# Attention, a ternary feed-forward and a channel mix in one launch: when stage one loads, sums and rounds its weights, and a loop in place of unrolled VectorE code

## The reference

```python
# x: (8, 512, 512), ctx: (8, 512, 384)
v = ln(x) @ Wv.T + bv;  t = ctx @ Wt.T + bt              # 512 x 256 each
x = x + (v @ t.T) / max(|v| |t|.T, 1e-8)                  # cosine attention
h = act_quant(ln(x)) @ ternary(w1).T                      # 512 -> 2048
h = silu(depthwise_conv3(h, conv_w) + conv_b)
x = x + act_quant(h) @ ternary(w2).T                      # 2048 -> 512
x = x + softmax_attention(ln(x), ctx)                     # 16 heads of 32
x = x + sigmoid(xr @ W_r.T) * (relu(xk @ W_k.T)**2 @ W_v.T)   # channel mix
```

## Time and profile before

| | us |
|---|---|
| median of 3 runs (1741.2 to 1742.52) | 1742.46 |
| the profiled execution: time | 1742.46 |
| its span, first to last instruction | 1740.7 |
| PE busy | 1591.3 (91%) |
| DVE busy | 1226.8 (70%) |
| ACT busy | 1159.6 (67%) |
| POOL busy | 1090.5 (63%) |
| mean granted TensorE clock, as a share of full speed | 0.975 |

### The profile page before, as it was taken

One profiled execution on the slowest core, in us unless ns is written; L12 is line 12 of the kernel. 1 busy time (PEld: TensorE's weight loads), 2 busy tenths in 40 slices (PEclk: granted clock), 3 DMA queues, 4 the chain that ended last, 5 costly groups with the idle time before them and its releaser, 6 DMA issues. The chain is left out here.

```text
span 1740.7 us, 29515 instructions
## 1 busy us (share of the span) xinstructions
PE 1591.3 (91%) x8932; PEld 718.5 (41%) x8932; DVE 1226.8 (70%) x1736; ACT 1159.6 (67%) x1915; POOL 1090.5 (63%) x786
## 2 busy tenths in 40 slices
PE   4989878998999977899999999999999978999998
PEld 2545433443444432334344444444443413444443
DVE  3888888988988755577686767676767674565553
ACT  4667598888888744665757666665757565656662
POOL 2767558888898833566757666675756673545452
PEclk9989999999999997999999999999999988999999
DMA  7321000000000113121211212121201100000001
GB/s 287 121 85 61 1 1 1 1 1 1 0 1 1 43 47 90 29 59 29 55 37 33 57 25 57 29 55 31 58 24 41 55 25 25 25 37 35 24 24 49
DMA packets 60464, 72.23 MB, mean 41 GB/s; under 512 B 14416, under 2 KB 40016, under 8 KB 59856
## 3 DMA queue, kind: packets, MB, share of 16 engines
q1 hardware_dynamic: 56944, 62.22, 12.1%
q10 hardware_dynamic: 3424, 8.91, 1.4%
HBM read 37.40 MB, written 8.39 MB: 26 GB/s over the span
## 5 line engine op out<-in xcount | busy, mean ns | idle before, releaser
L1540 DVE TENSOR_REDUCE s_mx<-bank 128x1 f32<-128x512 f32 x512 | 336.8, 685 | 199.9 <-PE bank L1672 194.1
L1425 ACT ACTIVATE s_E<-bank 128x512 f32<-128x512 f32 x512 | 293.5, 595 | 195.1 <-PE bank L1686 170.4
L1322 POOL TENSOR_TENSOR s_E<-s_E 128x1024 f32<-128x1024 f32 x128 | 300.4, 2366 | 121.5 <-PE bank L1694 113.8
L1672 PE MATMUL bank<-s_KA,s_QA 96*128 96x512 f16 x512 | 193.3, 388 | 16.9 <-DMA s_KA<-sm_cx 7.2
L1686 PE MATMUL bank<-s_QA,s_KA 97*128 97x512 f16 x512 | 196.0, 383 | 7.1 <-ACT s_E L1425 3.5
L1315 POOL TENSOR_TENSOR sm_cx<-s_qkf,sm_cx 128x512 f16<-128x512 f32 x64 | 76.4, 1194 | 175.0 <-ACT sm_cx L1403 174.1
L1694 PE MATMUL bank<-s_E,s_V 128*32 128x512 f32 x1024 | 138.0, 611 | 3.2 <-ACT s_E L1425 3.2
L1846 POOL TENSOR_TENSOR sm_cx<-m_xf,sm_cx 128x512 f16<-128x512 f32 x56 | 78.6, 1409 | 98.7 <-ACT sm_cx L1887 98.7
L1056 PE MATMUL bank<-sm_zz,w1raw 128*128 128x512 f16 x256 | 100.1, 391 | 27.0 <-DVE sm_cx L943 11.1
L1079 PE MATMUL bank<-f_w2q,w2raw 128*128 128x512 f16 x512 | 122.0, 379 | 1.4 <-ACT w2raw L824 0.6
L758 POOL TENSOR_TENSOR w1raw<-w1raw,sm_cx 128x512 f32<-128x512 f32 x88 | 121.0, 1384 | 2.3 <-ACT sm_cx L841 2.3
(11 more groups left out here) (262 smaller groups left out, 4116.9 us busy)
## 6 DMA issues: line engine op xcount, KB each, us to landing
sm_cx<-in_ctx SPq DMA_DIRECT2D x16, 768.0 KB, 4.6
s_QA<-sm_cx SPq DMA_DIRECT2D x384, 32.0 KB, 1.9
s_KA<-sm_cx SPq DMA_DIRECT2D x372, 32.0 KB, 1.9
X<-in_x SPq DMA_DIRECT2D x8, 1024.0 KB, 6.5
out_x<-X SPq DMA_DIRECT2D x8, 1024.0 KB, 4.3
w1raw<-in_w ACTq DMA_DIRECT2D x1, 4096.0 KB, 13.4
w2raw<-in_w ACTq DMA_DIRECT2D x1, 4096.0 KB, 28.3
w1raw<-in_wq SPq DMA_DIRECT2D x1, 1024.0 KB, 6.1
```

Source lines behind the costliest of these rows:

```text
L1322: e.tensor_tensor(into, into, other, ALU.add).then_inc(s_sum.sem, 1)
L1425: e.activation(E[:, SLOT[k] + h, :], SC[u % 2][:, :], ACT.Exp, scale=1.0 / float(np.sqrt(DH)))\
L1540: e.tensor_reduce(mx[:, q, h:h + 1], MX[q % 2][:, :], AX.X, ALU.max).then_inc(s_red.sem, 1)
L1672: e.matmul(MX[k % 2][:, :], QA[0:MROW, m, h, q * P:(q + 1) * P], KA[0:MROW, m, h, :], start=True, stop=True).then_inc(s_mx.sem, 1)
```

## The change

In `cosine_attention`: `cw` and `cb` are no longer loaded by SP at the start but by ACT, behind w1 and w2, and they count on w1's semaphore, so that every sum over w1 waits for 64 in place of 32. The sums are dealt out differently: one quarter of w1 in batch 0 (before two), one quarter and two eighths of w2 in batch 1, two quarters of w1 in batch 2. So w1's total falls to batches 2 and 3, and `weight_scale(0)` with `conv_scales` to batch 3, ahead of the first `quantised`. The statistics of the feed-forward's first batch move from the end of batch 2 to the end of batch 1. In batch 7 `rescale` moves from DVE to POOL (behind `split`, ahead of `add`), and ACT does two of its four `rescaled` behind `root_v`. In `softmax_attention` DVE's batches 1 to 6 become a loop.

```diff
-        SUMS = {0: ((0, 0), (0, 1)), 1: ((0, 2), (0, 3)), 2: ((1, 0),), 3: ((1, 1),), 4: ((1, 2),), 5: ((1, 3),),
-                6: ((1, 4),), B - 1: ((1, 5), (1, 6), (1, 7))}
-        QUANT, STATS_AT = {3: 0, 4: 1, 5: 2, 6: 3}, 2
+        SUMS = {0: ((0, 0),), 1: ((0, 1), (1, 0), (1, 1)), 2: ((0, 2), (0, 3)), 3: ((1, 2),), 4: ((1, 3),), 5: ((1, 4),),
+                6: ((1, 5),), B - 1: ((1, 6), (1, 7))}
+        QUANT, STATS_AT = {3: 0, 4: 1, 5: 2, 6: 3}, 1
...
-        s_raw, LOADED = [sem(f"raw{i}") for i in range(2)], 32
+        s_raw, LOADED = [sem(f"raw{i}") for i in range(2)], (64, 32)
...
-            e.dma_start(cw[:, :], cw_d).then_inc(s_bias, 16)      # SP
-            e.dma_start(cb[:, :], cb_d).then_inc(s_bias, 16)
...
+            e.dma_start(cw[:, :], cw_d).then_inc(s_raw[0], 16)    # ACT, behind w1 and w2
+            e.dma_start(cb[:, :], cb_d).then_inc(s_raw[0], 16)
...
+                else:                                             # POOL, batch 7
+                    for q in range(TT):
+                        rescale(q)
                 add(b)
...
-                    for q in range(TT):                           # ACT, batch 7
-                        rescaled(q)
+                    rescaled(0)
+                    rescaled(1)
                 root_v(b)
...
+                    rescaled(2)
+                    rescaled(3)
...
-                    e.wait_ge(s_raw[i], LOADED)                   # DVE, weights(b)
+                    e.wait_ge(s_raw[i], LOADED[i])
...
-                if b == 2:
-                    weight_scale(0)
-                    conv_scales()
                 if b in QUANT:
+                    if QUANT[b] == 0:
+                        weight_scale(0)
+                        conv_scales()
                     quantised(QUANT[b])
                 weights(b)
-                if b == 1:
+                if b == 2:
                     total(0)
...
-                    if b == 2 and i == 0:                         # PE
+                    if b == 3 and i == 0:
                         total(0)
...
-            steps(step, e, unrolled=True)                         # softmax_attention, DVE
+            steps(step, e)
```

More of the change, by code:

```diff
@@ L304, in centre, with rescale @@
                 e.tensor_scalar(nmr[:, :], nmr[:, :], -1.0, None, ALU.mult).then_inc(s_nmr.sem, 1)
+            def rescale(q):
+                s_r1.wait(e, 0, q + 1)
+                e.tensor_scalar(z[:, q, :], z[:, q, :], ROUND, rs1[:, q:q + 1], ALU.subtract, ALU.mult)\
+                    .then_inc(s_r2.sem, 1)
             ln_p(e, 0)
@@ L371, in _ @@
             context(0)
-            e.wait_ge(s_bias, 64)
+            e.wait_ge(s_bias, 32)
             def rescaled(q):
@@ L432, in total @@
             def total(i):
-                e.wait_ge(s_ws, PARTS[0] if i == 0 else sum(PARTS) + 1)
+                e.wait_ge(s_ws, PARTS[0] + 2 if i == 0 else sum(PARTS) + 1)
                 lo = i * PARTS[0]
@@ L451, in quantised @@
                 piece = raw[0][:, i * F:(i + 1) * F]
-                e.wait_ge(s_ws, PARTS[0])
+                e.wait_ge(s_ws, PARTS[0] + 2)
                 e.tensor_scalar(piece, piece, wr[:, 0:1], 1.0, ALU.mult, ALU.min).then_inc(s_wt, 1)
@@ L464, in token_scales @@
                 e.reciprocal(s1[:, :], rs1[:, :]).then_inc(s_am.sem, 1)
[L466 to L469, removed]
             def low_f(c):
@@ L478, in reciprocals @@
                 e.reciprocal(NT[:, :], nt[:, :]).then_inc(s_rec.sem, 1)
-                if b == B - 1:
-                    for q in range(TT):
-                        rescale(q)
                 s_root.wait(e, b, 2)
@@ L580, in norms_v @@
                     s_sq.wait(e, b, 2 * KH)
-                    if b == 2:
+                    if b == 3:
                         e.wait_ge(s_wm, 1)
@@ L600, in total @@
             def total(i):
-                e.wait_ge(s_ws, sum(PARTS) + 2 if i else PARTS[0] + 1)
-                s_root.wait(e, B - 1 if i else 1, 2)
+                e.wait_ge(s_ws, sum(PARTS) + 2 if i else PARTS[0] + 3)
+                s_root.wait(e, B - 1 if i else 2, 2)
                 e.matmul(NV[:, 8 + i:9 + i], ones[:, :], totals[:, i:i + 1], start=True, stop=True).then_inc(s_wp, 1)
```

## The result

The changed kernel takes 1774.53 us (median of four runs, 1771.11 to 1775.8), the kernel before 1742.08 in the same session: 1.0184 times as long, 95% interval 1.0166 to 1.0202. That is +32.5 us where +12.6 was forecast, and outside the range of 1744 to 1763. The profiled execution of the changed kernel took 1776.33 us, with a span of 1774.5, 33.8 more than before.

A forecast was written before the change was run, and what follows sets the result against it. PE was taken as the bound in the softmax (busy 565 of 570 us), DVE mattering only through PE's timeline. 10.8 + 2.5 - 5.5 - 1.2 + 6.0 = +12.6 on 1742.46 gave 1755 us, range 1744 to 1763.

The forecast's parts named there:

- DVE's loop: Softmax attention: late waits on registers cost 0.14 us more each, 85 times; half taken, +6.0 us (0 to 11.9).
- rival 2: Softmax attention: the loop costs nothing, since PE's queue has other work at each late wait; 1749 us, chance 0.22.
- rival 3: Softmax attention: register counts for each reduce make DVE the bound, +15 us on the first terms, 1764 us; chance 0.1.
- cw and cb behind w2: Batch 0: cb lands near 49.9 us, so DVE's first sum and `reciprocals` come late, +10.8 us (9.9 to 11.6).
- The cover: Batch 0: DVE's 3.24 us wait for ACT ahead of `reciprocals`, which hid part of the sums, is gone.
- The clock behind that gap: After batch 0: PE stands still some 10 us, then runs at the low clock, +2.5 us (1.7 to 3.5).
- Statistics and sums: Batches 2 and 3: batch 2 becomes 21.6 us, batch 3 20.2 in place of 27.1; -5.5 us (-6.9 to -2.3).
- Batch 7: Attention block's end: DVE sheds four `rescale` of together 1.59 us to POOL, priced by `split`; -1.2 us (-1.6 to +0.5).
- The reading by the Trainium skill: Batch 7: by roughly line rate on GpSimd, `rescale` would cost less than `split`'s 1.15 us, making the term -1.6.
- The rule that the forecast cites for the order of the queue: Batch 0's loads: an SDMA engine consumes its ring in order, so the count for the small loads can't come early.

The follow-up runs named there:

- the pairs: Changed kernel with DVE's softmax loop over pairs of batches, two jumps back in place of five, the same register waits: 1762.99 us, 1.0135.
- the kernel in which DVE alone waits: Changed kernel with SP issuing the two small loads in their old place and DVE's first sum made to wait for w2's landing: 1775.45 us, 1.0197.
- the loops of memsets: Kernel before with added DVE loops of 32 to 384 memsets, four passes each in the first run, behind its last instruction; only gaps read, time not used.

## Why the prediction was wrong

By ratios the parts are: loop +18.6 (taken out) to +23.5 (alone), small loads +11.5, rescale +0.9, statistics -0.2 and -1.2; 30 to 36 us against +32.5 measured and +12.6 forecast. By the two traces they are +11.0 up to `reciprocals` of batch 0, +1.0 and -2.7 in batches 2 and 3, +1.5 in batch 7, +3.6 in the feed-forward and +19.3 in the softmax.

- **DVE's loop**, forecast +6.0 with 0 to 11.9: this is the step that failed. The price was taken from late waits inside the channel mix's loop, "0.14 us" each, 85 of them, and the jump back stood in the sum at nothing, without a reason. Late waits cost nothing here (0.48 and 0.49 us): in the channel mix another wait on a register stands between the late one and the instruction, and the row measured that one; ahead of `maximum` the late wait is the last. The five jumps cost 19.3 us in the trace. The first looped batch, with all the register waits and no jump behind it, was not longer than before, and the pairs cost two jumps' worth. So rival 2 was right on the waits, and neither it nor rival 3 named the jump. The channel mix's body has 96 instructions and jumps back in 0.2 to 0.3 us. The row to ask was elsewhere in the same trace: the feed-forward's loop on DVE, whose body has 394, showed 2.8 us between its jump back and the next instruction. The nearest row was nearest in kind of wait, not in length of body.
- **cw and cb behind w2**, forecast +10.8, measured +11.0 at `reciprocals`: the size and DVE's landing were right, but the chain named was one of two, and the one that ended first. "The two issues that ACT now does itself stand ahead of `project` 0, for which ACT has to wait for PE anyway: nothing" was wrong by 18.29 us of blocked ACT. Each chain costs the 11 us alone, so the miss doesn't show in the sum; that it doesn't is luck. The cover, ACT's wait for PE, ended near 29 us, not 40.
- **The clock behind that gap**, forecast +2.5: +1.0 where that gap exists (in the kernel in which DVE alone waits). In the changed kernel it doesn't: ACT holds PE back in the middle of batch 0 instead, and the low clock after 41.80 ran beside DVE's own wait.
- **Statistics and sums**, forecast -5.5: mechanism right, size wrong. Batch 2 took 21.2 us (forecast 21.6). Batch 3 was to be "an ordinary 20.2", but PE still waited 1.48 us for POOL there, and it took 21.1, or 24.4 where the clock fell all the same, as in the changed kernel's trace. And the base was one execution's batch 3 of 27.1 us, where the mean of ten traces is 25.7. The mean gain is 2.3 us, the forecast's lower bound.
- **Batch 7**, forecast -1.2: `split`'s 1.15 us was no measure for `rescale` on POOL. It took 1.99, above the bound of 1.5, and turned the sign: +0.9 alone by the times, +1.5 in the traces. The reading by the Trainium skill, "GPSIMD Engine Reference", section "Engine selection", which makes one-input work on GpSimd roughly line rate, goes further off: DVE did the same four in 1.59 us, POOL in 7.96.
- **The feed-forward's +3.6 us** was not in the sum and is most likely the clock, from execution to execution: over 20 traces of kernels with the same feed-forward it took 432.8 to 436.8 us, 432.8 in the first trace of the kernel before, 434.5 in the second. In the 17 traces up to 434.7 us 22 to 44 of its 1584 large fp16 matmuls ran at the low clock, in the three of 435.9 and more 51 to 58. Those three all have the changed attention block ahead, but so have others of 432.8 and 433.2, so a part of the change in it is not shown and not excluded.
- The rule that the forecast cites for the order of the queue, from the Trainium skill, "DMA: Bandwidth & Descriptors", section "Queues, rings and completion order", agrees: `cb` landed at 48.50, when w2 had. It says nothing that would have priced the issue on ACT.

Still open: what holds `cw`'s issue for 18.3 us (the number of pieces waiting, or their bytes) and from how much on; and whether POOL's 1.99 us comes of the two scalar operands or of the engine's load at the time.

## What to carry to other kernels

Before turning unrolled code on DVE into a loop, count the instructions of the body and look how the trace behaves behind the jump of a loop of like length; where it stops, either drop waits that an earlier wait covers, or shift the body by a few instructions, and look again whenever code ahead of it changes. Never put a small load behind large ones on the queue of an engine that has compute to do, even if nobody waits for the load: its issue waits, and the engine with it. And before a gain is computed from one slow stretch, look at a second trace of the same kernel.

## What the runs showed of the hardware

- DVE jumps back in about 0.3 us when the loop's body lies in at most three stretches of 128 instructions, and stops for 2.7 to 3.6 us when it lies in four. A second stop stands where the first stretch ends, until 3.3 to 4.5 us after the body's first instruction in the softmax (2.2 to 2.5 us in the loops of memsets), and is hidden where DVE is busy or waiting that long. A body of 369 instructions cost 23.5 us in five jumps or nothing, depending on 8 instructions ahead of it.
- Such a pass brings five more packets of instructions of 8 KB (79 against 54 packets, and 78 against 53, in five jumps).
- A run of memsets on DVE, one every 28 ns, stops for about 0.33 us every 128 instructions.
- The issue of a 24 KB load by ACT took 18.3 us behind two loads of 4 MB each and 0.41 us ahead of them; ACT began nothing in between.
- A `tensor_scalar` of 128x512 with two operations took 1.99 us on POOL and 0.40 on DVE; a subtraction of the same size on POOL 1.15.
